# Attention heads: where TensorE's transposition of the row maxima stands among the transposed score blocks

## What is computed

```python
att = jnp.einsum('bhcq,bhCq->bhcC', q, k) / d_query
causal = jnp.arange(T)[:, None] >= jnp.arange(T)[None, :]
att = jnp.where(causal, att, -jnp.inf)
p = jax.nn.softmax(att, axis=-1)
y = jnp.einsum('bhcC,bhCv->bhcv', p, v)
z = jnp.einsum('dvh,bhcv->bcd', W, y) * (math.sqrt(d_embed / d_value) / num_heads)
```

## Time and profile before

| | |
|---|---|
| median of 3 runs | 2085.6 us (2085.28 to 2085.81) |
| the profiled execution | 2088.93 us |
| its span | 2087.2 us |
| transpositions of the maxima (line 2495) | 64, from 609.7 to 1813.5 us of the span |
| TensorE busy in the span | 1831.8 us (88%) |

### The profile page before, as it was taken

How to read it: one execution, slowest core, us unless ns; L and a number is a source line. 1 busy time by engine, 2 the same in 40 slices (tenths; PEclk the granted TensorE clock), 3 DMA queues, 4 the chain that set the end, 5 groups by cost and what they waited for, 6 DMA issues and landing times. The chain is left out here.

```text
span 2087.2 us, 40578 instructions
## 1 busy us (share of the span) xinstructions
PE 1831.8 (88%) x12355; PEld 1436.0 (69%) x12356; DVE 1481.6 (71%) x3795; ACT 1138.1 (55%) x2322; POOL 1182.6 (57%) x1159
## 2 busy tenths in 40 slices
PE   5863899999599999999999999999999999973870
PEld 2552788888467777787777777777777777743650
DVE  7785677777657787757787757787757787663663
ACT  5331455556546566646656646656656656522760
POOL 4355233333216566636687836687836687835782
PEclk9856999999789999999999999999999999977995
DMA  9863433333321211212121111121111121123979
GB/s 340 256 208 105 104 56 55 54 54 55 85 89 52 59 52 52 60 31 54 55 80 48 49 29 55 52 60 52 45 29 54 52 60 53 30 96 90 202 122 264
DMA packets 215684, 177.34 MB, mean 85 GB/s; under 512 B 85442, under 2 KB 200727, under 8 KB 214880
## 3 DMA queue, kind: packets, MB, share of 16 engines
q1 hardware_dynamic: 177904, 138.78, 22.2%
q0 software_dynamic: 28656, 27.61, 8.5%
q10 hardware_dynamic: 8960, 8.92, 1.3%
HBM read 95.05 MB, written 80.72 MB: 84 GB/s over the span
## 5 line engine op out<-in xcount | busy, mean ns | idle before, releaser
L957 POOL TENSOR_TENSOR c_den_late<-c_den_late,c_p 128x512 f32<-128x512 f32 (+3 forms) x384 | 409.5, 1066 | 129.1 <-ACT c_p L1283 83.6
L1283 ACT ACTIVATE c_p<-PS 128x512 f32<-128x512 f32 (+3 forms) x768 | 343.3, 491 | 207.1 <-PE PS L2512 99.6
L2531 PE MATMUL PS<-c_p,c_vh 128*64 128x256 f32 (+3 forms) x3072 | 292.5, 332 | 0.5 <-ACT c_yT L1265 0.5
L2511 PE MATMUL PS<-c_q,c_k 128*128 128x512 f32 (+2 forms) x768 | 283.3, 373 | 3.2 <-ACT c_p L1283 1.6
L2488 PE MATMUL PS<-c_k,c_q 128*128 128x512 f32 (+2 forms) x768 | 268.9, 364 | 8.2 <-DVE c_max L1873 3.3
L2512 PE MATMUL PS<-c_q,c_k 128*128 128x512 f32 (+2 forms) x768 | 258.3, 348 | 0.0
L893 POOL DMA_INDIRECT acc<-b_y,b_tok x71 | 114.6, 1614 | 253.2 <-ACT b_y L1149 223.4
L2531 PEld LDWEIGHTS PS<-c_p,c_vh 128*64 128x64 f32 x3072 | 194.3, 136 | 87.8 <-issue 20.6
L1274 ACT ACTIVATE c_q<-PS 64x512 fp32r<-64x512 f32 x256 | 151.3, 591 | 159.0 <-PE PS L2475 155.8
L1873 DVE TENSOR_REDUCE c_max<-PS 128x1 f32<-128x512 f32 x256 | 175.4, 685 | 46.3 <-PE PS L2488 45.9
L957 POOL TENSOR_TENSOR c_den<-c_den,c_p 128x384 f32<-128x384 f32 (+2 forms) x192 | 141.9, 739 | 108.8 <-ACT c_p L1283 83.5
(11 more groups left out here) (313 smaller groups left out, 4342.7 us busy)
## 6 DMA issues: line engine op xcount, KB each, us to landing
c_vh<-c_v SPq DMA_DIRECT2D x64, 256.0 KB, 3.2
c_rrow<-rden SPq DMA_DIRECT2D x63, 256.0 KB, 3.4
routed<-b_empty SPq DMA_DIRECT2D x32, 289.0 KB, 9.5
d_xe<-routed SPq DMA_DIRECT2D x32, 289.0 KB, 4.1
b_xt<-routed SPq DMA_DIRECT2D x71, 130.0 KB, 2.1
b_w12T<-in_w12T_dram SPq DMA_DIRECT2D x16, 512.0 KB, 13.8
d_acc<-acc SPq DMA_DIRECT2D x16, 512.0 KB, 9.0
c_st_hi<-wqk_split SPq DMA_DIRECT2D x48, 128.0 KB
```

Of the source, the lines that this page charges most:

```text
L957: pool.tensor_tensor(den[:, off:], den[:, off:], p, ALU.add).then_inc(s_cPa, 1)
L1283: act.activation(c_p[:, P_AT[h][m]:P_AT[h][m] + WIDTH[m]], PS[:, ST_BANK[m % STB], skip:skip + WIDTH[m]], ACT.Exp, scale=ATT_SCALE).then_i ...
L2511: pe.matmul(PS[:, bank, 0:n], c_k1[h][:, j * P:(j + 1) * P], c_q1[h][:, q], start=True, stop=False)
L2531: ins = pe.matmul(dst, c_vh[h][:, j, :], columns[:, :, a, :], start=(j == 0), stop=(t0 == 3))
```

## The change

In `head_products` the transposition of the next head's maxima is issued behind the transposed blocks 9 and 10, and ahead of block 11, where it was issued ahead of all three. Nothing is added or removed, and the orders of VectorE, ScalarE, GpSimd and SP are the same as before.

```diff
@@ head_products
                 outputs_of(1)
+                for m in (9, 10):
+                    scores_t(H, h, m)
                 if follows:
                     transpose_max(H + 1, table)
-                for m in (9, 10, 11):
-                    scores_t(H, h, m)
+                scores_t(H, h, 11)
                 mask_t(9, 10, 11)
```

## The result

| | before | changed |
|---|---|---|
| median, four runs each, us | 2085.7 (2085.28 to 2089.06) | 2099.0 (2095.98 to 2101.74) |
| the profiled execution, its time and its span, us | 2088.93, 2087.2 | 2095.98, 2094.2 |

The changed kernel is slower: the ratio is 1.006, with a 95% interval from 1.0042 to 1.0077, so 13.3 us, with an interval from 8.8 to 16.1. The forecast was 2096.5, 10.9 above the median before.

A forecast was written before the change was run, and what follows sets the result against it. PE's own order was taken to bound the attention heads. Plain heads 11.1, held heads 0.2, the late-landing head 0.2, last head 0.7, late maxima -1.3 sum to +10.9 us: 2096.5 us, range 2090 to 2103.

The forecast's parts named there:

- plain heads: Heads where PE's own order sets the time; 41 were to lose 0.27 us each, 11.1 us.
- rival (c): No difference: later waits in plain heads give back the 0.27 us; 2085 to 2089 us, chance 0.11.
- The chain: Transposition, ScalarE's copy, DMA issue and landing, to next head's block 0: 2.44 us, against 0.36 us of slack.
- Rival (d): Faster: chain at most 2.13 us, only the transposition's wait for VectorE goes; 2079.7 us, chance 0.05.
- Rival (b): DMA landing slower at its new time, every fifth late by 1.08 us; 2105 us, chance 0.06.
- wrong in mechanism: The prediction's verdict on itself if block 0 still has no idle time before it in the changed kernel.
- The open load behind a wait: Block 0's weight load cannot start early behind the DMA wait: 0.11 us more per plain head.
- T's place: Transposition between full-width blocks: 0.01 us added; one more open weight load could bring a plain head's loss to 0.37.
- Rival (a): Loss paid everywhere and slot dear: 0.30 to 0.37 us in 55 heads; 2102 to 2106 us, chance 0.16.
- three pairs at the late maxima: Later sequences' heads where the transposition waits 0.9 us for VectorE's last maximum: gain 0.42 each, -1.3 us counted.
- 14 held heads: Heads where PE is held later, so a loss at block 0 costs nothing: +0.2 us all together.
- the head at 1466.78: Its DMA landed 0.55 us late, yet the time came back in a later VectorE wait; counted +0.2 us.

The follow-up runs named there:

- with three blocks: Changed kernel with the transposition behind blocks 9, 10 and 11, ahead of the masks: 2128.05 us, ratio 1.0111 to the kernel before.
- the pair without the landing: Old and changed orders, maxima sent to spare memory, block 0 not waiting, exponential's scale a hundredth: 2102.27 us old order, 2106.27 us changed order.
- the run with only the late heads: Kernel before, transposition behind blocks 9 and 10 only in the six heads where it waited for VectorE: 2101.87 us, ratio 0.999.

## Why the prediction was right

**The bound.** It said that PE's own order sets the time and that in the plain heads no other engine's work would cover the loss. They show it: 32 heads of that kind lose 9.9 us together. So rival (c), the loss given back there too, fell.

**The chain.** 2.44 us from T to block 0 was taken from the last head alone. It is 2.45 in the changed kernel, in its last head, and with three blocks. Rival (d) wanted at most 2.13 and fell. Rival (b), a slower landing at the new time, fell too: four of the 64 DMAs landed 0.4 to 0.6 us late (T at 642.45, 957.85, 1399.95 and 1714.89), not every fifth by 1.08. The same four heads are late in the second trace of this kernel and in the run with only the DMA late, which speaks for something at these places in the kernel; no row says what. The sign that the prediction named, idle time before block 0 that names the DMA, stands at block 0's weight load (0.16 us) and, but for five heads, not at its matmul. Whoever had looked at the matmul's row alone would have read "wrong in mechanism". The Trainium skill (DMA: Bandwidth & Descriptors, Anatomy of one DMA) has about 2.0 us of fixed cost, and it has it for DMAs that GpSimd issues, a limit that the prediction left out; this row of 4 KB within SBUF, issued by the SP queue, took 1.85 from its issue to the matmul that waited.

**The open load behind a wait.** Forecast 0.11, measured 0.10 to 0.11, in the changed kernel and in the run with only the DMA late. The Trainium skill (TensorE: Matmul & The Clock Gate, Step-by-step: what each phase is for) says that PE pulls weight loads ahead of running matmuls; the trace agrees where nothing is waited for (0.17 us ahead), and behind the wait the load starts with its matmul.

**T's place.** The forecast was 0.01, with up to 0.37 for the head if one more load stood open. One does, and T's place costs 0.10, as the pair without the landing shows. The sentence that this doesn't come on top, since PE waits for the DMA anyway, held in the plain heads: block 0 comes 2.45 us behind T whatever stands between the two, so the open load behind T is taken out of the wait. Of the 0.27 to 0.28 that such a head lost, 0.10 is T's place, 0.07 the wait and 0.10 the open load behind it, where the forecast had 0.15 to 0.16 of wait and 0.11 of load. Rival (a) was right that the slot is dear, and wrong that this adds to the landing. But in the heads that another engine holds a little behind block 0, the place is all that is paid, and that wasn't in the sum.

**Which heads pay.** Here the sum was right by errors that cancel. From the run of the changed kernel again, against before:

| heads | forecast, us | measured, us |
|---|---|---|
| plain, 32 | 8.6 (0.27 each) | 10.0 (0.25 to 0.34 each, and 0.92 in one with a late landing) |
| nine more, counted as plain | 2.4 | 0.85 (0.10 each) |
| three pairs at the late maxima | -1.3 | 0.1 |
| three with the wait for `c_yT` | about 0.2 | -0.7 |
| first sequence | about 0.2 | -0.9, of which some -1.3 is the odd head of before |
| last head | 0.7 | 0.6 to 0.7 |
| sum | 10.9 | 10.0; about 11.3 without the odd head |

The rows of the forecast are its terms put to these heads; its +0.2 for 14 held heads is spread over the third to fifth. Six of the nine are held at block 1 by ScalarE's exponential of block 0 (1.0 us in six in PE's list of waits before), three by `c_xT_lo`. In such a head a later block 0 shortens the wait, and T's place stays. That row of 1.0 us is missing in the earlier trace rows, as is another (line 1916 for VectorE's `X`, 1.0 us in three). Both are longer than its fifth row, so the five longest entries come to 14.9 us and not to 14.7, and the two matter: the late maxima's gain went into the second.

The first failed step is "In the three later ones I count it, -1.3 us": T's wait for VectorE gave way, and VectorE's next late result took its place. That same reasoning stood in the prediction for the head at 1466.78, and it should have been applied here. For the first sequence it was applied, and there three heads gained 1.6 us in the run with only the late heads. The head that was to show how VectorE holds that sequence, 16.56 us, isn't of the kind that takes 15.60: its counterparts in the later sequences take 16.89. The second is the `c_yT` heads: they gained 0.2 us each, and the `c_yT` wait went from PE's list. That this is T's shift handing VectorE a little time is a guess; no run separates it.

So the forecast's 10.9 is close to the measured 13.3 and 10.8 partly by luck: the chain and the plain heads were understood, and the terms for the other heads were wrong by up to some 1.5 us each, with opposite signs.

**What stays open.** The first runs and the later ones give 13.3 us (8.8 to 16.1) and 10.8 (7.8 to 14.3 from the ratio's interval), which overlap. The profiled executions explain some 11.

## What to carry to other kernels

A DMA that nothing waits for has a slack that its row doesn't show. Find one execution of the same chain where the waiting engine has nothing else to do (here the last head), take its length from there, and subtract: 0.36 us of slack against a move of 0.68 decided this change.

A wait on TensorE costs its length and the weight load that could not start early, here 0.10 us, and neither need show as idle time of the matmuls; the weight loads' own rows have the wait. A tiny matmul between two full-width ones costs a load as well. The one cheap place that these runs show is the old one, behind the outputs; behind the masks, where a load stands open too, it cost the head the same 0.10 us.

The largest entry of the waits isn't a gain to be had. Where VectorE was busy 92% of the stretch, the wait came back at the next result that it owed; where it was busy 80%, 1.6 us of a possible 2 were gained.

## What was not expected of the hardware

An 8-column weight load with a 128-column matmul takes 0.03 us by itself between two blocks, and makes the pair behind it 0.08 us longer: the next matmul's weight load isn't hidden by so short a one. Behind the outputs, whose weights have 64 columns, the same transposition costs 0.01 us.

From issue to the waiting matmul the DMA took 1.85 us at each place that the rows show, whether it was issued 0.60 or 1.24 us behind T. Four or five of 64 came later than that, by 0.3 to 1.0 us over three traces, and four heads are late in all three.
